# Sums of state products in quads instead of pairs, in the last stage of a two-layer GNN and Mamba kernel

## What is computed

```python
h = maximum(layernorm(x), 0); x = x + relu((D^-1/2 adj D^-1/2 @ h) @ W.T + b)          # layer 0
h = maximum(layernorm(x), 0); x = x + mamba(layernorm(relu(adj @ h @ gcn_w + gcn_b)))  # layer 1
```

```python
dA = exp(dt[:, :, None] * A[None]); dBu = dt[:, :, None] * B[:, None, :] * u[:, :, None]
hst = dA[t] * hst + dBu[t];  ys[t] = hst @ C[t]          # for t = 0 .. 8191
y = (ys + u * D_skip) * silu(z);  return y @ w_out
```

## Time and profile before

| | |
|---|---|
| time, median of 3 runs | 2681.08 us (2680.63 to 2681.3) |
| profiled execution, own time | 2687.66 us |
| its span, first to last instruction | 2685.8 us |
| TensorE busy | 2325.4 us (87%) |
| VectorE busy | 2082.0 us (78%) |
| ScalarE busy | 979.5 us (36%) |
| GpSimd busy | 936.9 us (35%) |
| mean granted clock of TensorE | 0.954 |

### The profile page before, as it was taken

One profiled execution on the slowest core, in us unless ns is written; L12 is line 12 of the kernel. 1 busy time (PEld: TensorE's weight loads), 2 busy tenths in 40 slices (PEclk: granted clock), 3 DMA queues, 4 the chain that ended last, 5 costly groups with the idle time before them and its releaser, 6 DMA issues.

```text
span 2685.8 us, 22298 instructions
## 1 busy us (share of the span) xinstructions
PE 2325.4 (87%) x7072; PEld 1314.6 (49%) x7072; DVE 2082.0 (78%) x2079; ACT 979.5 (36%) x1696; POOL 936.9 (35%) x409
## 2 busy tenths in 40 slices
PE   0347688999999999999999989999999989997776
PEld 0113344444447888888885444444444444443333
DVE  5888888886645666566652599999999899999997
ACT  0000000000004555555552455555545555555552
POOL 0000000000000000000000388777778788787554
PEclk9978789999999999999999999999999999998898
DMA  8999999898766555555547655555555555551121
GB/s 337 380 398 412 394 393 388 356 404 321 263 247 236 214 214 216 197 213 196 199 183 266 231 198 210 207 208 204 198 211 213 197 207 206 204 196 63 67 75 52
DMA packets 108325, 643.02 MB, mean 239 GB/s; under 512 B 14225, under 2 KB 15025, under 8 KB 42673
## 3 DMA queue, kind: packets, MB, share of 16 engines
q1 hardware_dynamic: 92160, 604.02, 59.3%
q10 hardware_dynamic: 16048, 37.57, 4.0%
HBM read 625.28 MB, written 16.25 MB: 239 GB/s over the span
## 4 chain that ended last, share of the span: by engine, by line
PE 57%; DVE 28%; issue 8%; ACT 3%; ACTq 1%; DMA 1%; DVEq 0%; POOL 0%; SPq 0%; POOLq 0%
PE ps L813 21%; PE ps L731 13%; DVE arena L550 11%; PE ps L853 10%; DVE arena L664 6%; DVE ps L653 6%; PE ps L890 4%; PE ps L928 4%; PE ps L753 2%; ACTq L958 1%; DMA diag_h<-adj 1%; PE ps L874 1%; PE ps L909 1%; DVE ring L664 1%; PE ps L932 1%
## 5 line engine op out<-in xcount | busy, mean ns | idle before, releaser
L813 PE MATMUL ps<-adj_parts,h_parts 128*128 128x512 f32 x2592 | 593.7, 391 | 2.5 <-ACT adj_parts L1024 2.2
L442 POOL TENSOR_TENSOR rstd<-base,minus_half 128x8 f32<-128x8 f32 (+1 forms) x40 | 84.7, 2118 | 1450.7 <-DVE base L490 877.9
L853 PE MATMUL ps<-ring,diag_h 128*128 128x512 f32 x1152 | 549.0, 611 | 0.3 <-DVE arena L640 0.2
L458 POOL TENSOR_TENSOR arena<-arena 128x1024 f32<-128x1024 f32 x192 | 458.5, 2394 | 251.1 <-ACT state L1091 251.1
L813 PEld LDWEIGHTS ps<-adj_parts,h_parts 128*128 128x128 f32 x2592 | 485.0, 188 | 108.6 <-ACT adj_parts L1024 4.7
L550 DVE TENSOR_TENSOR arena<-arena,ring 128x2048 f32<-128x2048 f32 x208 | 476.8, 2292 | 67.0 <-DMA ring<-adj 49.2
L731 PE MATMUL ps<-ring,arena 128*128 128x512 f32 x928 | 437.7, 633 | 62.4 <-DMA ring<-adj 62.4
L664 DVE TENSOR_TENSOR_SCAN arena<-arena,state,ps 128x512 f32<-128x512 f32 x384 | 470.6, 1267 | 26.1 <-DVE ps L653 1.0
L853 PEld LDWEIGHTS ps<-ring,diag_h 128*128 128x128 f32 x1152 | 223.8, 196 | 252.4 <-issue 249.3
L1099 ACT ACTIVATE arena<-arena,a_sb 128x512 f32<-128x512 f32 x512 | 338.3, 708 | 0.4
L577 DVE TENSOR_TENSOR adj_parts<-ring,adj_parts 128x1024 fp32r<-128x1024 f32 x216 | 264.0, 1224 | 94.3 <-ACT adj_parts L1024 83.5
(11 more groups left out here) (85 smaller groups left out, 1783.1 us busy)
## 6 DMA issues: line engine op xcount, KB each, us to landing
ring<-adj SPq DMA_DIRECT2D x480, 1024.0 KB, 6.5
arena<-c_scratch SPq DMA_DIRECT2D x128, 512.0 KB, 3.8
diag_h<-adj SPq DMA_DIRECT2D x32, 1024.0 KB, 12.2
arena<-x ACTq DMA_DIRECT2D x16, 512.0 KB, 4.7
x_scratch<-arena ACTq DMA_DIRECT2D x8, 512.0 KB, 3.0
arena<-x_scratch ACTq DMA_DIRECT2D x16, 256.0 KB, 4.3
out<-arena ACTq DMA_DIRECT2D x16, 256.0 KB, 3.0
lower_scratch<-arena ACTq DMA_DIRECT2D x7, 512.0 KB, 2.6
```

Of the source, the lines that this page charges most:

```text
L458: nc.gpsimd.tensor_tensor(buf, buf, c_row, ALU.mult).then_inc(mult_done, 1)
L813: last = nc.tensor.matmul(acc[:, c, :], h_parts[:, blk % 2, layer, h_part, a * F:(a + 1) * F], adj_parts[:, buf, adj_part, c * MM:(c + 1) ...
L853: last = nc.tensor.matmul((acc_c if i else y_ps)[:, c, :], tile_of(h1, JT * s + a), blk[:, a * STRIP + c * MM:a * STRIP + (c + 1) * MM], s ...
```

## The change

GpSimd adds, after the second pair of four states, the two pair sums (a quad), for the 13 chunks in which it added pairs. TensorE adds a quad at the seventh step after its first state (QSUM = 7: steps 7, 11, 15 of a chunk and step 3 of the next) instead of a pair at every even step, so four terms a chunk instead of eight. The last three chunks keep both terms of each pair. There are ten state buffers instead of eight, and the ring has five buffers in stage C instead of six. VectorE waits, before it writes a buffer again, for the quad add where the buffer is not the one that holds the quad's sum, and otherwise for TensorE.

```diff
--- before.py
+++ after.py
@@ -40,7 +40,7 @@
 MM = 512
 
 RING = 7
-RING_C = 6
+RING_C = 5
 
 T = 512
 NCH = N // T
@@ -58,7 +58,7 @@
 LN_EPS = 1e-5
 DEG_EPS = 1e-9
 
-HSB = 8
+HSB = 10
 
 AHEAD = 12
 
@@ -67,7 +67,7 @@
 GCN, BIAS, STATS, POWER, NORMALISE = -19, -19, -17, -17, -15
 TRANSPOSE, XZ, SILU, DBC, SPLIT = -13, -12, -7, -6, -5
 DT, SOFTPLUS, WEIGHTED_U = -4, -3, -1
-NSUM = 6
+QSUM, NSUM = 7, 6
 LOAD_X1, SKIP, GATE, OUT, RESIDUAL = 12, 20, 21, 25, 25
 
 
@@ -234,9 +234,10 @@
         dt = [work2(HALVES, T) for _ in range(2)]
         w = [work2(HALVES, T) for _ in range(2)]
         da = [work2(HALVES, T) for _ in range(2)]
-        hs = [work2(HALVES, T) for _ in range(HSB - 2)]
-        hs += [ring[:, RING - 1, b * HALVES * T:(b + 1) * HALVES * T].rearrange("p (a b) -> p a b", a=HALVES)
-               for b in range(2)]
+        hs_pairs = [work2(2 * HALVES * T) for _ in range(HSB // 2 - RING + RING_C)]
+        hs_pairs += [ring[:, r, :] for r in range(RING_C, RING)]
+        hs = [hs_pairs[b // 2][:, b % 2 * HALVES * T:(b % 2 + 1) * HALVES * T].rearrange("p (a b) -> p a b", a=HALVES)
+              for b in range(HSB)]
         csb = [work2(2, T) for _ in range(2)]
         yg = work2(HALVES, T)
         x1t = work2(CT, F)
@@ -335,6 +336,7 @@
         state_saved = sem("state_saved")
         mult_done = sem("mult_done")
         pair_done = sem("pair_done")
+        quad_done = sem("quad_done")
         nsum_done = sem("nsum_done")
         y_free = sem("y_free")
         yg_ready = sem("yg_ready")
@@ -361,7 +363,14 @@
 
             eng.wait_ge(misc_free, misc_at[kind, k] + 1)
 
-        PAIRS_ADDED = (NCH - SPARED) * (DS // 2)
+        QUADS = DS // 4
+        QUAD_CHUNKS = NCH - SPARED
+
+        def sums(k, n):
+
+            if k < QUAD_CHUNKS:
+                return QUADS * k + n // 4 + 1
+            return QUADS * QUAD_CHUNKS + DS // 2 * (k - QUAD_CHUNKS) + n // 2 + 1
 
         weight_loads = [
             (ident[:, :], ident_in), (w0t_sb[:, :], w0t), (b0_sb[:, :], b0.to_broadcast([P, F])),
@@ -456,10 +465,14 @@
                     pool.wait_ge(c_in[g // 2 % 2], 16 * (g // 4 + 1))
                     c_row = csb[g // 2 % 2][:, g % 2:g % 2 + 1, :].to_broadcast([P, HALVES, T])
                     nc.gpsimd.tensor_tensor(buf, buf, c_row, ALU.mult).then_inc(mult_done, 1)
-                    if g % 2 and g // 2 < PAIRS_ADDED:
+                    if g % 2 and g < QUAD_CHUNKS * DS:
                         pool.wait_ge(mult_done, g + 1)
                         even = hs[(g - 1) % HSB]
                         nc.gpsimd.tensor_tensor(even, even, buf, ALU.add).then_inc(pair_done, 1)
+                        if g % 4 == 3:
+                            pool.wait_ge(pair_done, g // 2 + 1)
+                            first = hs[(g - 3) % HSB]
+                            nc.gpsimd.tensor_tensor(first, first, even, ALU.add).then_inc(quad_done, 1)
 
 
         @block.vector
@@ -658,7 +671,11 @@
                         dve.wait_ge(state_saved, g - DS + 1)
                     if g >= HSB:
 
-                        dve.wait_ge(nsum_done, (g - HSB) // 2 + 1)
+                        k_old, n_old = divmod(g - HSB, DS)
+                        if k_old < QUAD_CHUNKS and n_old % 4:
+                            dve.wait_ge(quad_done, (g - HSB) // 4 + 1)
+                        else:
+                            dve.wait_ge(nsum_done, sums(k_old, n_old))
                     dve.wait_ge(dbu_done, g + 1)
                     for h in range(HALVES):
                         nc.vector.tensor_tensor_scan(hs[g % HSB][:, h, :], da[g % 2][:, h, :], dbu_ps[g % 2][:, h, :],
@@ -698,7 +715,7 @@
                     nc.vector.tensor_tensor(w[k % 2], dt[k % 2], u[k % 2], ALU.mult).then_inc(w_ready, 1)
                 k = chunk_at(g, SKIP)
                 if k is not None:
-                    dve.wait_ge(nsum_done, DS // 2 * (k + 1))
+                    dve.wait_ge(nsum_done, sums(k, DS - 1))
                     if k:
                         dve.wait_ge(misc_full, misc_at["out", k - 1] + 1)
                     for h in range(HALVES):
@@ -873,23 +890,26 @@
                     pv = parts[kk % 2]
                     nc.tensor.matmul(b_ps[(g + 1) % 2], pick[:, nn:nn + 1].to_broadcast([KP, P]), pv[0:KP, :],
                                      start=True, stop=True).then_inc(b_ready, 1)
+                q, odd = divmod(g - QSUM, 4)
+                if not odd and 0 <= q < QUAD_CHUNKS * QUADS:
+                    pe.wait_ge(quad_done, q + 1)
+                    if q % QUADS == 0 and q:
+                        pe.wait_ge(y_free, q // QUADS)
+                    for h in range(HALVES):
+                        last = nc.tensor.matmul(y_ps[:, h, :], ident[:, :], hs[4 * q % HSB][:, h, :],
+                                                start=q % QUADS == 0, stop=q % QUADS == QUADS - 1)
+                    last.then_inc(nsum_done, 1)
                 G, odd = divmod(g - NSUM, 2)
-                if not odd and 0 <= G < NCH * DS // 2:
-
+                if not odd and QUAD_CHUNKS * DS // 2 <= G < NCH * DS // 2:
                     pair = G % (DS // 2)
-                    terms = [hs[2 * G % HSB]]
-                    if G < PAIRS_ADDED:
-                        pe.wait_ge(pair_done, G + 1)
-                    else:
-                        pe.wait_ge(mult_done, 2 * G + 2)
-                        terms.append(hs[(2 * G + 1) % HSB])
-                    if pair == 0 and G:
+                    pe.wait_ge(mult_done, 2 * G + 2)
+                    if pair == 0:
                         pe.wait_ge(y_free, G // (DS // 2))
-                    for j, term in enumerate(terms):
+                    for j in range(2):
                         for h in range(HALVES):
-                            last = nc.tensor.matmul(y_ps[:, h, :], ident[:, :], term[:, h, :],
+                            last = nc.tensor.matmul(y_ps[:, h, :], ident[:, :], hs[(2 * G + j) % HSB][:, h, :],
                                                     start=pair == 0 and j == 0,
-                                                    stop=pair == DS // 2 - 1 and j == len(terms) - 1)
+                                                    stop=pair == DS // 2 - 1 and j == 1)
                     last.then_inc(nsum_done, 1)
                 k = chunk_at(g, GCN)
                 if k is not None:
```

## The result

The changed kernel takes 2652.14 us (median of 4 runs, 2651.2 to 2652.91) against 2680.98 us; the ratio is 0.9889, with a 95% interval of 0.9877 to 0.9902. That is -28.8 us where the prediction had -12: the direction was right, the size was not.

The account below looks back on a forecast made before the run. In the last stage TensorE and VectorE, coupled step by step, were taken to bound the kernel. Relief of -25 us and meetings of +13 us gave -12 us, 2669 us for the median; range 2646 to 2688.

Parts of the forecast that it names:

- What bounds the kernel: Last stage, eleven chunks (the stretch): TensorE costs VectorE 32.6 us of waits, 3.0 a chunk, all that relief can buy.
- Meetings: VectorE's GATE, SPLIT and variance meeting GpSimd instructions: 1.0 us a chunk more waiting, +13 us, ends 0 and 27.
- With GpSimd almost never idle: VectorE starting at a random point of a 2.36 us GpSimd instruction waits 1.18 us, three 3.5: 1.6 us a chunk more.
- Identity matmuls: TensorE's sums, 416 instructions down to 208: 1.93 us a chunk less VectorE waiting, 25 us over 13 chunks, ends 0 and 39.
- The walk through steps 3 to 9: TensorE's piled-up steps in one chunk: output product's 1.60 us wait falls to some 0.35, broadcast's 1.57 goes.
- the change moves nothing there: Step 13, TensorE at the dt product waiting for VectorE's BIAS, 27.8 us, next broadcast queued behind: unchanged.
- 3.0 instead of 10: VectorE's wait for the broadcast of B (L874), 17.4 us in eleven chunks: 10 taken to go, ends 0 and 17.4.
- The clock rival: TensorE, less busy, spends more time at 1.2 GHz; half of the 25 us comes back, 2681 us; chance 0.06.
- GpSimd's adds fit: 52 more adds, 9.8 us a chunk; GpSimd would need 68.4 of about 73 us and fits.
- nothing to spare: GpSimd's gaps in the chunk shown: some 4.9 us carried into the last gap of 5.05.
- Ring and buffers: Ring of five and ten state buffers in the last stage: 0 us.
- The lock: VectorE–GpSimd port rule: three VectorE instructions could each lose a whole GpSimd instruction, +42 us, 2723; chance 0.02.

Follow-up runs that it names:

- the relief alone: Changed kernel without the quad add, TensorE taking only the first pair of each quad (half the state sum left out in 13 chunks): 2645.34 us, ratio 0.987.
- BIAS is moved: Changed kernel with GCN and BIAS one step later (step 14 instead of 13): 2636.36 us, and again 2633.62 us.
- three quads of four: Changed kernel with GCN and BIAS one step later and states 8 to 11 added as pairs by TensorE: 2620.48 us, ratio 0.9773.

## Why the prediction was wrong

*What bounds the kernel*: right. The stage alone decides, most of the gain came through VectorE's waits for TensorE, and it was far below the 89 us of TensorE work taken away.

*Meetings*, +13 us: this is the step that failed. The forecast had them 11 us dearer in the stretch; they got 4.7 us cheaper. Carried over to 13 chunks, that difference is some 18.5 us, and the forecast was off by 16.8. Two things were wrong in it. The adds themselves cost less than 13 us: 4.0 alone, 6.8 beside the relief, where the three groups rise from 35.7 to 40.5 us. And the sum has no term for the relief's own effect on the meetings: a VectorE that comes earlier meets GpSimd elsewhere, -9.5 us in the stretch by the relief alone. The stated range's lower end, 2646, still held the time.

"With GpSimd almost never idle" a random start was assumed, or three distances read off one chunk that I had shifted. The starts are not random. A chunk repeats itself with a period of 71.5 us in the mean (70.1 to 73.2), and each of the three instructions tends to fall at its own point of GpSimd's sequence: 5 of 11 SPLITs started 0.43 or 0.44 us before an end, and GATE and variance have nearly one duration in most chunks. In the kernel before, the reason can be read from the trace: what each of the 11 GATEs meets, and each of the 9 SPLITs that meet anything, is a multiply that had stood waiting for the state that a scan had just left, so GpSimd's start and VectorE's both count from the scans, and GATE comes 1.98 or 1.99 us after the multiply's start in 9 of the 11 chunks. In the changed kernel GATE keeps such a distance (1.9 us after the quad add's start in 9 of 11) though GpSimd stood waiting for nothing just before; what holds it there was not found.

*Identity matmuls*, 25 us, which is 21.3 in the stretch: the waits fell by 20.3, TensorE's by 16.3 and the exponential's by 4.0. So this term was of the right size, in part by luck, since its parts were not. The walk through steps 3 to 9 held for the output product (11.3 us forecast; 13.3 measured) and for the broadcast of step 8, for which VectorE waited 9.8 us in the stretch and now does not wait (1.7 us came new in step 9). It failed for the broadcast that VectorE needs in step 15, of which it said "the change moves nothing there": the wait grew from 5.8 to 10.9 us. In the same step the scan's wait for the exponential fell from 13.5 to 9.4; the one wait stands in front of the other, and together they went from 19.4 to 20.3 us, so neither the "3.0 instead of 10" for L874 nor the -4.0 is a loss or a gain by itself. Behind the pause for BIAS (27.8 to 32.2 us) TensorE was at half clock before the change too: from the dt product to VectorE's multiply of step 15 for 26 us in all, in 8 of the 11 chunks, and for 40 us, in 10 of 11, after it. The chunks without half clock there have no such wait. The clock rival had this mechanism and gave it half of the whole gain; the two waits of step 15 together grew by only 0.9 us in the stretch.

*GpSimd's adds fit*: right, with 96% of the stretch busy and no wait for a quad. The slack was larger than "nothing to spare": one more add a chunk costs 7 us and does not make it the bound, four more do, at 89 us above the changed kernel where 92 were worked out in advance.

*Ring and buffers*, 0: right, 1.0005 by themselves.

*The lock*: by the rule of the Trainium skill (SBUF — State Buffer, "SBUF: two separate sides") a VectorE instruction with two SBUF inputs waits until the GpSimd instruction that holds the ports is over, and the other way round. The runs agree with it: GATE ended 1.09 us after the quad add, an instruction put in front of SPLIT was free as long as SPLIT still started before GpSimd's end, and a SPLIT that started just after the next one had begun waited up to 2.1 us. The variance (L490, L503) waits in the same way with one SBUF input and constants, which is not the case of two inputs that the prediction took from the rule. That each would lose a whole instruction every time is not what happens.

Open: the adds cost 7 us beside the relief and 20 after BIAS is moved. The durations show where (the variance 1.9 against 15.8 us, GATE 13.2 against 19.4), and the trace shows what is in the way, a multiply begun 0.3 us earlier; why the loop settles there is not shown. Nothing was tried that keeps the order of GpSimd's work and shifts it alone.

## What to carry over

Relief of an engine in a lockstep is worth the waits that it removes, found step by step, and not its share of busy time. Add up waits that stand one in front of the other in the same step before calling one of them a gain. Look also at where the relieved engine pauses for another: in 10 of 11 chunks here TensorE ran at half clock behind its 2.9 us pause, and moving the work that it paused for by one step gave as much as the change itself.

Where VectorE's instructions wait for GpSimd's, as three of them do here, GpSimd's busy share does not give the price of more work on it. The same 52 adds cost 4, 7 and 20 us, by where in a GpSimd instruction each of the three starts, and a change anywhere in the loop moves that, by -10 to +10 us in eleven chunks here. So it can pay to give up a part of such a change: three quads of four beat all four by 12 to 13 us.

## What the runs showed of the hardware

A VectorE instruction held up by GpSimd ends at a fixed distance from GpSimd's end: SPLIT 0.55 us, whether it had waited 0.3 or 2.1 us, GATE 1.08 or 1.09 us and the variance 0.03 us. A SPLIT that starts 0.1 us after the beginning of a GpSimd instruction waits for all of it (2.8 us instead of 0.69), one that starts 0.1 us before its end for almost nothing (0.69 to 0.70 us). GpSimd pays as well: the multiply that starts while a held-up GATE still runs takes 3.34 us instead of 2.35 (in ten of the changed kernel's eleven chunks), and behind a SPLIT 2.8. TensorE, which had paused 2.9 us in chunk 5, was granted 0.50 of its clock in the next 3.3 us, in which it was busy for 3.1, and six matmul instructions took 4.06 us instead of 2.74.
